# The last pair's feed-forward cut into two units, an earlier position table, masks that open the score banks, and new engine orders

## The chip, the cores and the metric

The kernel runs on one core of a Trainium2 chip. Its metric is the device time of one execution in microseconds (us); lower is better. A core has five engines that matter here, each with its own in-order instruction queue: TensorE (PE; its weight loads are shown as PEld), VectorE (DVE), ScalarE (ACT), GpSimd (POOL) and SyncE (SP), which only issues DMAs in this kernel. They meet through semaphores. PSUM has eight banks, into which PE writes and from which DVE and ACT read.

## The reference

Sixteen images of 3x96x96 are cut into 36 patches of 16x16, each projected to 256 features; with a class token and position embeddings this makes 37 tokens. 128 text tokens are appended: 165 tokens a sequence. Then one transformer block follows:

```
h = concat([cls, patches @ W_lin.T + b]) + pos ; h = concat([h, txt])      # (16, 165, 256)
# attention: 16 query heads, 4 key/value heads of 16; rope; |i - j| <= 32 only
h = h + softmax(mask(rope(q) @ rope(k).T / 4)) @ v @ Wo                    # on layernorm(h)
# feed-forward, both matmuls with per-token int8 activations and ternary weights
u = bit_linear(layernorm(h), w1)                                          # 256 -> 1024
u = silu(depthwise_conv1d(u, conv_w, conv_b))                             # 3 taps along the sequence
h = h + bit_linear(u, w2)                                                 # 1024 -> 256
```

The convolution couples each token of a sequence with its two neighbours; nothing couples two sequences. The second `bit_linear` scales each token by the largest of its 1024 values, so its down projection can only start when all 1024 features of the token are known.

## The kernel before

Two sequences make a pair: `T` = 330 tokens, as three tiles of `TT` = 110 rows. There are eight pairs (`PAIRS`). For each pair `n` the attention runs in 11 blocks `j` of 30 queries (`QB`): `scores` (two fp32r matmuls, L1817, and a bf16 mask matmul onto the edge columns, L1829, the last of the three), `max_s` on DVE (L1488), `shift` (L1837, subtracts the maximum), `exp` on ACT (L1259), `turn_p` (four transposes, L1846), `keep_p` on ACT (L1267) and `context` (eight matmuls into 32-column tiles, L1860). Two PSUM banks (`S_BANKS`) alternate over the blocks. After 4, 8 and 11 blocks, `turn_ctx`, `norm`, `select`, `keep_sel` and `out_proj` (L1887) make one tile of 110 tokens, and `add_att` adds it to `h` (L1504).

The feed-forward of pair `n` is: `var2`, `rstd2`, `norm2`, `max_x`, `quant_x`, `dequant_x` (normalise and quantise three tiles), `turn_xs` (six transposes), `high_x`, `low_x` (the operand as two fp32r halves), then eight chunks `m` of 128 hidden features: `up` (four matmuls of 330 columns, L1915 and L1916), `mid` on ACT (centre tap and bias, L1306), `left` and `right` on DVE (the outer taps, L1564 and L1571). Per four chunks: `tanh` on ACT, `silu` (L1578), `abs_g` on ACT, `fold_g` (L1588), `max_g`. Then `turn_max` (L1922), `scale2`, `spread` (L1927, the scale of each token to all partitions), `quant_g` (L1625, int8), `conv_g` on ACT (int8 to bf16, L1326), `down` (8 matmuls a tile, L1934), `add_ffn` (L1633) and `store`.

For pairs 0 to 6 `up` uses three banks in turn and `down` the same three, one a tile. The last pair uses four others for `up`, so that it need not wait for the banks; its `turn_xs` goes to `F_BANK` and `N_BANK`. `up` of chunk m waits until `right` of the chunk that had its bank before is done.

The order of the work on each engine is not worked out at run time. `ORDER` holds for every helper, pair and piece a tick; each engine runs its helpers by rising tick, in order. An item with a late tick sits behind all items with earlier ones, and what it waits for stalls all behind it. The feed-forward of pair n is interleaved in this way with the attention of pair n+1; the last pair's has nothing beside it but what is left of pair 6's. `ONCE` does the same for the start: the images' transposes (`turn_pix`), the patch projections (`patch`: 12 matmuls L1715 and one L1717 with the position table) and the weights' quantisation.

`patch(0)` stands behind a wait for `consts_in`, the DMA of all constants but the identity (132.5 KB). The last 164 of its columns, from `C_HOT`, are the one-hot rows that pick a position's row of `posb`.

Of the kernel before, what the change touches and what calls it, by code (L numbers as in the profile page):

```python
# [37 lines left out]
NT = 3  # L38
# [11 lines left out]
HALFC = MH // 2  # L50
K_PLACED = 16 * 2 * HKV
# [66 lines left out]

C_ID = 0
# [8 lines left out]
for _j in range(NB):  # L128
    if V_RUNS:
# [14 lines left out]
        (19, 21),  # L144
        (69, 73),
        (137, 142),
        (219, 223),
        (294, 300),
        (374, 381),
        (451, 454),  # L150
    ),
    'pe.project': (
        (7, 8, 10),
        (23, 28, 36),
        (77, 82, 89),
        (155, 159, 166),
        (230, 236, 243),
        (308, 312, 316),
        (384, 390, 399),
        (462, 469, 475),  # L160
    ),
    'pe.turn_q': (
        (12, 14, 17),
        (43, 51, 57),
        (106, 115, 125),
        (178, 187, 197),
        (257, 265, 278),
        (334, 344, 355),
        (408, 422, 430),
        (490, 498, 510),  # L170
    ),
    'pe.turn_k': (
        (15, 16),
        (60, 65),
        (129, 135),
        (201, 206),
        (284, 290),
        (361, 367),
        (440, 445),
        (513, 518),  # L180
    ),
    'pe.scores': (
# [8 lines left out]
    ),  # L191
    'pe.shift': (
# [8 lines left out]
    ),  # L201
    'pe.turn_p': (
# [8 lines left out]
    ),  # L211
    'pe.context': (
# [29 lines left out]
    'pe.out_proj': (
        (55, 79, 96),
        (124, 156, 172),
        (200, 225, 249),
        (276, 304, 327),
        (356, 380, 404),
        (433, 457, 480),
        (509, 538, 556),
        (578, 599, 609),  # L250
# [3 lines left out]
        (204,),  # L254
        (280,),
        (358,),
        (436,),
        (514,),
        (583,),
        (613,),  # L260
    ),
    'pe.up': (
# [8 lines left out]
    ),  # L271
    'pe.turn_max': (
        (176,),
        (253,),
        (328,),
        (406,),
        (484,),
        (558,),
        (610,),
        (624,),  # L280
# [3 lines left out]
        (260,),  # L284
        (337,),
        (413,),
        (492,),
        (563,),
        (611,),
        (625,),  # L290
    ),
    'pe.down': (
        (193, 194, 195),
        (270, 271, 272),
        (349, 350, 351),
        (425, 426, 428),
        (503, 504, 505),
        (572, 573, 574),
        (612, 614, 615),
        (626, 627, 628),  # L300
# [3 lines left out]
        (8,),  # L304
        (13,),
        (17,),
        (40,),
        (101,),
        (149,),
        (198,),  # L310
# [40 lines left out]
    ),  # L351
    'dve.norm': (
        (23, 34, 41),
        (48, 56, 82),
        (93, 106, 129),
        (142, 156, 180),
        (194, 203, 227),
        (240, 251, 277),
        (288, 298, 324),
        (337, 346, 367),  # L360
    ),
    'dve.add_att': (
        (29, 37, 44),
        (52, 76, 86),
        (100, 117, 135),
        (150, 176, 184),
        (200, 223, 233),
        (247, 271, 281),
        (295, 320, 330),
        (343, 361, 370),  # L370
# [3 lines left out]
        (87,),  # L374
        (136,),
        (185,),
        (234,),
        (282,),
        (332,),
        (372,),  # L380
# [3 lines left out]
        (94,),  # L384
        (143,),
        (192,),
# [3 lines left out]
        (377,),  # L390
    ),
    'dve.low_x': (
        (55,),
        (102,),
        (151,),
        (201,),
        (248,),
        (297,),
        (345,),
        (382,),  # L400
    ),
    'dve.left': (
# [8 lines left out]
    ),  # L411
    'dve.right': (
# [8 lines left out]
    ),  # L421
    'dve.silu': (
        (68, 79),
        (119, 128),
        (167, 178),
        (216, 226),
        (263, 275),
        (312, 322),
        (363, 369),
        (401, 402),  # L430
    ),
    'dve.fold_g': (
        (77, 83),
        (126, 132),
        (171, 181),
        (224, 230),
        (272, 279),
        (323, 327),
        (368, 373),
        (403, 405),  # L440
    ),
    'dve.max_g': (
        (81, 84),
        (130, 133),
        (174, 182),
        (228, 231),
        (274, 280),
        (325, 329),
        (371, 374),
        (404, 406),  # L450
    ),
    'dve.scale2': (
        (88,),
        (137,),
        (186,),
        (235,),
        (284,),
        (331,),
        (376,),
        (407,),  # L460
    ),
    'dve.quant_g': (
# [1557 lines left out]
```

## Time and profile before

| | |
|---|---|
| median of 3 runs | 415.74 us (414.12 to 416.45) |
| profiled execution, whole | 415.2 us |
| its span, first to last instruction | 413.4 us |
| busy | PE 352.1, DVE 304.9, ACT 256.1, POOL 213.2 us |
| mean granted TensorE clock | 0.94 of 2.4 GHz |

A group's mean duration of a matmul covers its whole way through the array; matmuls overlap, so the distance from one start to the next is what one costs in a stream. The slices of the page are a fortieth of the span each, some 10.3 us.

### The profile page before, as it was taken

The numbers are of one execution on the slowest core, as the hardware profiler recorded it, in microseconds if no ns is written. First come the engines' busy times: TensorE is split into PE (matmuls) and PEld (weight loads), VectorE is DVE, ScalarE is ACT, GpSimd is POOL, SyncE is SP. The second block draws the span as 40 slices with busy tenths as digits, with TensorE's granted clock in tenths as the row PEclk, the third lists the DMA queues.
The fourth block names the chain that finished last, engine by engine and source line by source line (L and its number), as shares of the span: only waits on it lengthen the run. The fifth ranks groups of instructions, "written<-read, shape, count | busy, mean of one in ns | idle before, by whom it ended". The sixth has DMA issues, their size and how long they took to land.

```text
span 413.4 us, 8175 instructions
## 1 busy us (share of the span) xinstructions
PE 352.1 (85%) x2920; PEld 270.8 (66%) x2920; DVE 304.9 (74%) x644; ACT 256.1 (62%) x481; POOL 213.2 (52%) x245
## 2 busy tenths in 40 slices
PE   1698789999999999999999999999999989737424
PEld 1375546777876796678667866896688667517304
DVE  2246567664699788878978899589869986985971
ACT  2222435658795788578767894788678765813721
POOL 5407489489559917981899059926960052010000
PEclk9979999999999999999999999999999999955956
DMA  7671601101100121012001201110111001000101
GB/s 238 147 178 41 215 19 33 33 11 26 22 14 2 32 52 32 2 36 55 11 1 25 61 18 32 35 27 9 32 36 35 0 2 35 0 0 2 33 1 33
DMA packets 21884, 16.69 MB, mean 40 GB/s; under 512 B 12413, under 2 KB 20914, under 8 KB 21843
## 3 DMA queue, kind: packets, MB, share of 16 engines
q1 hardware_dynamic: 20948, 15.11, 14.8%
q10 hardware_dynamic: 895, 1.06, 1.0%
q8 instruction: 23, 0.38, 0.4%
q14 instruction: 18, 0.15, 0.1%
HBM read 9.82 MB, written 3.38 MB: 32 GB/s over the span
## 4 chain that ended last, share of the span: by engine, by line
PE 68%; DVE 14%; ACT 8%; issue 6%; DMA 2%; ACTq 0%; DVEq 0%
PE bank L1817 7%; PE bank L1846 7%; PE bank L1766 6%; PE bank L1934 6%; PE bank L1860 6%; PE bank L1915 5%; PE bank L1715 4%; PE bank L1887 4%; PE bank L1916 4%; PE bank L1837 3%; PE bank L1878 2%; DMA cst<-in_consts 2%; DVE shared L1625 2%; PE bank L1829 2%; PE bank L1927 2%
## 5 line engine op out<-in xcount | busy, mean ns | idle before, releaser
L1267 ACT COPY pT<-bank 94x480 f32<-94x480 f32 (+3 forms) x88 | 48.4, 554 | 28.9 <-PE bank L1846 28.1
L1488 DVE TENSOR_REDUCE mx<-bank 120x4 fp32r<-120x376 f32 (+3 forms) x88 | 44.2, 505 | 29.9 <-PE bank L1829 29.2
L1817 PE MATMUL bank<-kbd,q_hl 128*120 128x376 f32 (+3 forms) x176 | 50.8, 373 | 5.9 <-ACT pT L1267 3.3
L1259 ACT ACTIVATE pr<-bank 120x376 f32<-120x376 f32 (+3 forms) x88 | 39.6, 455 | 25.3 <-PE bank L1837 24.6
L1846 PE MATMUL bank<-cst,pr 120*94 120x120 f32 (+3 forms) x352 | 51.1, 269 | 2.7 <-ACT pr L1259 2.2
L1107 POOL TENSOR_TENSOR rs<-ve,half_neg 110x3 f32<-110x3 f32 x16 | 16.6, 1040 | 65.1 <-DVE ve L1516 48.0
L1915 PE MATMUL bank<-xT_hi,w1T 128*128 128x330 f32 x128 | 42.9, 341 | 1.1 <-DVE late L1571 0.9
L1846 PEld LDWEIGHTS bank<-cst,pr 120*94 120x94 f32 (+3 forms) x352 | 36.3, 121 | 11.1 <-ACT pr L1259 6.7
L1129 POOL TENSOR_TENSOR rc<-qk,cst 110x320 f32<-110x320 f32 x22 | 20.7, 939 | 43.7 <-ACT qk L1230 42.7
L1114 POOL TENSOR_SCALAR xn<-h,mv,rs 110x256 f32<-110x256 f32 x21 | 26.5, 1272 | 26.5 <-PE bank L1754 26.1
L1916 PE MATMUL bank<-xT_lo,w1T 128*128 128x330 f32 x128 | 39.4, 314 | 0.0
L1860 PE MATMUL bank<-pT,vw 94*32 94x120 f32 (+3 forms) x704 | 37.4, 291 | 1.5 <-ACT pT L1267 1.4
L1837 PE MATMUL bank<-mx,neg_id 120*120 120x376 f32 (+3 forms) x88 | 36.2, 417 | 2.8 <-DVE mx L1488 2.4
L1766 PE MATMUL bank<-wqk,xnT 128*110 128x384 f32 x96 | 37.0, 510 | 0.3 <-ACT xnT L1223 0.3
L1817 PEld LDWEIGHTS bank<-kbd,q_hl 128*120 128x120 f32 x176 | 26.1, 182 | 15.8 <-ACT pT L1267 6.9
L1934 PE MATMUL bank<-w2T,shared 128*110 128x256 bf16 x192 | 26.9, 303 | 9.4 <-ACT shared L1326 9.4
L1934 PEld LDWEIGHTS bank<-w2T,shared 128*110 128x110 bf16 x192 | 24.7, 147 | 11.9 <-ACT shared L1326 11.6
L1326 ACT CAST shared<-shared 128x1320 bf16<-128x1320 int8 x16 | 20.4, 1296 | 16.7 <-DVE shared L1625 16.4
L1136 POOL TENSOR_TENSOR qkr<-rc,rsn 110x160 f32<-110x160 f32 x44 | 29.7, 695 | 1.7
L1860 PEld LDWEIGHTS bank<-pT,vw 94*32 94x32 f32 (+3 forms) x704 | 19.0, 146 | 17.7 <-issue 10.9
L1164 POOL TENSOR_SCALAR shared<-shared,am 110x256 f32<-110x256 f32 x21 | 23.8, 1144 | 5.6 <-ACT shared L1287 5.6
L1156 POOL TENSOR_SCALAR shared<-h,mv,rs 110x256 f32<-110x256 f32 x21 | 25.9, 1241 | 1.2 <-POOL rs L1107 1.1
(126 smaller groups left out, 863.9 us busy)
## 6 DMA issues: line engine op xcount, KB each, us to landing
out<-h SPq DMA_DIRECT2D x8, 330.0 KB
kbd<-shared SPq DMA_DIRECT2D x56, 41.2 KB, 2.1
wn<-in_w SPq DMA_DIRECT2D x2, 1024.0 KB, 6.6
shared<-in_x SPq DMA_DIRECT2D x4, 432.0 KB
h<-in_txt SPq DMA_DIRECT2D x1, 770.0 KB
late<-in_lin SPq DMA_DIRECT2D x1, 768.0 KB, 7.2
vw<-v_rows SPq DMA_DIRECT2D x8, 94.0 KB
v_rows<-qk SPq DMA_DIRECT2D x8, 82.5 KB
```

The lines of the kernel that those rows point to most:

```text
L1136: o = nc.gpsimd.tensor_tensor(qkr[:, e::2], rc[:, e::2], rsn[:, 1 - e::2], ALU.add)
L1259: nc.scalar.activation(pr[:, g % 3, 0:HKV * WIDTH[j]], S_BANKS[g % 2][0:QP, 0:HKV * WIDTH[j]], ACT.Exp, scale=HD ** -0.5).then_inc(exped, 1)
L1267: nc.scalar.copy(pT[0:WIDTH[j], g % 3, :], S_BANKS[g % 2][0:WIDTH[j], 0:HKV * QP]).then_inc(p_kept, 1)
L1488: nc.vector.tensor_reduce(mx[:, g % 4, :].bitcast(F32R), S_BANKS[g % 2][0:QP, 0:HKV * WIDTH[j]].rearrange("p (k c) -> p k c", k=HKV), axis ...
L1766: o = nc.tensor.matmul(qk_bank(n, t)[0:TT, 0:QKC + QK], xnT[:, k, t * TT:(t + 1) * TT], wqk[:, k, :], start=(k == 0), stop=(k == KD - 1))
L1817: nc.tensor.matmul(dst, q_hl[n % 2][:, j * QB:(j + 1) * QB, :].bitcast(F32R), kbd[n % 2][:, part, :, k0:k0 + w].bitcast(F32R), start=(part ...
L1837: nc.tensor.matmul(S_BANKS[g % 2][0:QP, 0:HKV * w], neg_id[:, :].bitcast(F32R), mx[:, g % 4, :].bitcast(F32R).unsqueeze(2).to_broadcast([Q ...
L1846: o = nc.tensor.transpose(S_BANKS[g % 2][0:w, kv * QP:(kv + 1) * QP], pr[:, g % 3, kv * w:(kv + 1) * w], ident[0:QP, 0:QP])
L1860: o = nc.tensor.matmul(C_BANK[VS * kv:VS * (kv + 1), col:col + QP], vw[n % 2][0:WIDTH[j], j, :, kv], pT[0:WIDTH[j], g % 3, kv * QP:(kv + 1 ...
L1915: nc.tensor.matmul(dst, w, xT_hi[:, k, :].bitcast(F32R), start=(k == 0), stop=False)
L1916: o = nc.tensor.matmul(dst, w, xT_lo[:, k, :].bitcast(F32R), start=False, stop=(k == KD - 1))
L1934: o = nc.tensor.matmul(down_bank(n, t)[0:TT, 0:D], gq[:, m, t * TT:(t + 1) * TT], w2T[:, m, :], start=(m == 0), stop=(m == MH - 1))
```

## The change

- `UNITS` = 9: pairs 0 to 6 are units 0 to 6; the last pair is units 7 and 8. Unit 7 is its first sequence: it normalises and quantises tiles 0 and 1 (220 tokens), computes `up` for 166 columns (165 and one more), convolves, gates and takes maxima over 165 tokens, and scales and quantises tile 0 (110 tokens). Unit 8 is the second: tile 2 is normalised, `up` again covers 166 columns, the gate 165 tokens, and tiles 1 and 2 (220 tokens) are quantised. All three `down` of the pair stay behind unit 8's `spread` in PE's order; the first waits only for unit 7's casts, the others for unit 8's.
- Banks: `up` of unit 6 has two banks instead of three, `down` of pair 6 uses two in turn, unit 7 has two banks (one of them `F_BANK`), unit 8 three. Units 7 and 8 turn their operands, maxima and scales in one bank each (`F_BANK`, `N_BANK`).
- Unit 7's normalisation and quantisation of two tiles is on POOL and ACT; before, the last pair's was on DVE.
- The last pair is stored tile by tile.
- `scores`: the mask matmul comes first and opens the bank (`start=True`), the two score matmuls add to it.
- The one-hot columns have a DMA of their own (37 rows of 656 bytes), second on ACT's queue; `patch` waits for it instead of `consts_in`.
- All of `ORDER` and `ONCE` are new.

```diff
-            pe.wait_ge(consts_in, 16)
+            pe.wait_ge(hot_in, 16)
...
             act.dma_start(cst[:, 0:C_REST], ident_d).then_inc(ident_in, 16)
+            act.dma_start(cst[0:POSR, C_HOT:C_END], hot_d).then_inc(hot_in, 16)
             act.dma_start(posb[:, :], pos_d).then_inc(pos_in, 16)
             act.dma_start(clsb[:, :, :], cls_d).then_inc(cls_in, 16)
-            act.dma_start(cst[:, C_REST:C_END], consts).then_inc(consts_in, 16)
+            act.dma_start(cst[:, C_REST:C_HOT], consts).then_inc(consts_in, 16)
...
+def tiles_of(u):
+    return range(NT) if u < LAST else (range(0, 2), range(2, NT))[u - LAST]
+def conv_of(u):
+    return (0, T) if u < LAST else ((0, SEQ), (SEQ, T))[u - LAST]
+def up_of(u):
+    return (0, T) if u < LAST else ((0, SEQ + 1), (SEQ - 1, T))[u - LAST]
+def gate_tiles(u):
+    return range(NT) if u < LAST else (range(0, 1), range(1, NT))[u - LAST]
...
-        def up_bank(n, m):
-            return Z_BANKS[m % 3] if n < PAIRS - 1 else (*S_BANKS, C_BANK, Z_BANKS[2])[m % 4]
+        def up_banks(u):
+            if u < LAST - 1:
+                return Z_BANKS
+            return (Z_BANKS[0:2], (Z_BANKS[2], F_BANK), (*S_BANKS, C_BANK))[u - LAST + 1]
...
         def down_bank(n, t):
-            return Z_BANKS[t] if n < PAIRS - 1 else (*Z_BANKS[0:2], S_BANKS[0])[t]
+            return Z_BANKS[t % 2 if n == LAST - 1 else t]
...
-                for part in range(2):
-                    nc.tensor.matmul(dst, q_hl[n % 2][:, j * QB:(j + 1) * QB, :].bitcast(F32R),
-                                     kbd[n % 2][:, part, :, k0:k0 + w].bitcast(F32R), start=(part == 0), stop=(part == 1))
...
                 nc.tensor.matmul(over, identb[0:QP, 0:QP], hide,
-                                 start=False, stop=True, skip_group_check=True).then_inc(scored, 1)
+                                 start=True, stop=False, skip_group_check=True)
+                for part in range(2):
+                    o = nc.tensor.matmul(dst, q_hl[n % 2][:, j * QB:(j + 1) * QB, :].bitcast(F32R),
+                                     kbd[n % 2][:, part, :, k0:k0 + w].bitcast(F32R), start=False, stop=(part == 1),
+                                     skip_group_check=True)
+                o.then_inc(scored, 1)
...
             def down(n, t):
-                pe.wait_ge(g_kept, NP * (n + 1))
-                if n == PAIRS - 1:
+                if n < LAST:
+                    pe.wait_ge(g_kept, NP * (n + 1))
+                    if n == LAST - 1 and t == 2:
+                        pe.wait_ge(ffn_added, NT * n + 1)
+                else:
+                    pe.wait_ge(g_kept, NP * (LAST + min(t, 1) + 1))
                     pe.wait_ge(ffn_added, NT * n)
...
+            def store_tile(t):
+                sp.wait_ge(ffn_added, NT * LAST + t + 1)
+                sp.dma_start(out_v[LAST][:, t, :], h[:, LAST, t, :]).then_inc(stored, 16)
```

The end of the new orders, by tick (in brackets the unit or pair and the piece). ACT: ... tanh(6,1), quant_x(7), keep_sel(7,2), abs_g(6,1), high_x(7), mid(7,0), mid(7,1), conv_g(6,0), conv_g(6,1), ... DVE: ... norm(7,2), fold_g(6,0), left(6,6), left(6,7), right(6,6), right(6,7), max_x(7), max_g(6,0), silu(6,1), add_att(7,2), var2(8), fold_g(6,1), max_g(6,1), norm2(8), low_x(7), scale2(6), left(7,0), max_x(8), quant_g(6,0), quant_g(6,1), ... PE: ... up(6,6), context(7,10), turn_ctx(7,2), up(6,7), select(7,2), out_proj(7,2), turn_xs(7), turn_max(6), up(7,0), up(7,1), spread(6), up(7,2), up(7,3), down(6,0), turn_xs(8), ... At the start, PE's `turn_pix` of the fourth load comes right after `turn_xn(0)`; before, three items later.

## Rows read from the trace of the kernel before

**Rows 1.** The page's slices: granted TensorE clock, tenths, 40 equal slices.
```profile
PEclk9979999999999999999999999999999999955956
```

**Rows 2.** Windows: per stretch the length, then each engine's busy us, PEclk, DMA share.
```profile
60.00:345.00 285.00, 273.51 (x2486) 213.32 (x2486) 229.06 (x476) 207.41 (x398) 182.35 (x209) 1.00 0.11 26
345.80:390.10 44.30, 28.44 (x186) 22.68 (x184) 37.01 (x81) 22.72 (x35) 1.40 (x1) 0.77 0.03 9
371.00:381.00 10.00, 6.14 (x31) 6.14 (x32) 6.03 (x12) 3.35 (x4) 0.00 (x0) 0.51 0.01 2
390.10:413.40 23.30, 6.80 (x29) 5.17 (x29) 11.90 (x18) 6.49 (x5) 0.00 (x0) 0.59 0.05 15
```

**Rows 3.** Waits of PE from 60 to 345 us: total us, times, longest.
```profile
PE bank L1817 <- ACT pT L1267: 2.6, 7, 0.6
PE bank L1837 <- DVE mx L1488: 2.4, 6, 0.7
```

**Rows 4.** The chain that ended last, at the start: start, us, what.
```profile
1.98 9.74 DMA cst<-in_consts
```

**Rows 5.** Timeline of DVE, 0 to 40 us: start, us, line, shapes, idle before.
```profile
8.89 0.92 DVE L1393 COPY wn<-bank 128x144 f32<-128x144 f32 x3 [2.03 <-PE bank L1702]
...
18.33 0.95 DVE L1388 COPY shared<-shared 72x768 f32<-72x768 f32 x1 [2.52 <-DMA shared<-in_x]
19.35 0.92 DVE L1393 COPY wn<-bank 128x144 f32<-128x144 f32 x3
```

**Rows 6.** Timeline of PE, 34 to 41 us.
```profile
37.14 2.83 PE L1715 MATMUL bank<-late,wn 128*126 128x256 f32 x12 [1.10 <-issue]
```

**Rows 7.** Timeline of PE in the body, two stretches.
```profile
60.68 0.44 PE L1860 MATMUL bank<-pT,vw 94*32 94x120 f32 x8
61.05 1.54 PE L1766 MATMUL bank<-wqk,xnT 128*110 128x384 f32 x4
...
115.99 0.65 PE L1860 MATMUL bank<-pT,vw 94*32 94x120 f32 x16
116.57 0.49 PE L1817 MATMUL bank<-kbd,q_hl 128*120 128x248 f32 x2
```

**Rows 8.** Groups by form, weight loads: busy us, mean ns, idle before.
```profile
L1817 PEld LDWEIGHTS bank<-kbd,q_hl 128*120 128x120 f32 x176 | 26.1, 182 | 15.8 <-ACT pT L1267 6.9 <-issue 4.0 <-ACT q_hl L1236 2.0
L1829 PEld LDWEIGHTS bank<-mask_sb,identb 120*120 120x120 bf16 x88 | 11.6, 132 | 0.0
```

**Rows 9.** Groups by form, DVE.
```profile
L1564 DVE SCALAR_TENSOR_TENSOR shared<-bank,conv,shared 128x328 f32<-128x328 f32 x32 | 17.2, 553 | 2.9 <-ACT shared L1306 2.8
L1578 DVE SCALAR_TENSOR_TENSOR late<-wn,late 128x1320 f32<-128x1320 f32 x8 | 12.2, 1539 | 0.0
```

**Rows 10.** Timeline of all engines, last pair's attention end and first `up`.
```profile
362.92 0.42 DVE L1504 TENSOR_TENSOR h<-bank,h 110x256 f32<-110x256 f32 x1 [0.77 <-PE bank L1887]
...
380.88 0.40 PE L1915 MATMUL bank<-xT_hi,w1T 128*128 128x330 f32 x1
```

**Rows 11.** Timeline of all engines, from the last `right` to the last addition.
```profile
389.11 1.01 DVE L1571 SCALAR_TENSOR_TENSOR late<-bank,conv,late 128x328 f32<-128x328 f32 x2
...
396.41 0.89 PE L1922 MATMUL bank<-cst,shared 128*110 128x128 f32 x3 [8.61 <-DVE shared L1599]
...
398.90 1.47 PE L1927 MATMUL bank<-shared,ones 110*128 110x330 f32 x2 [1.60 <-DVE shared L1615]
400.40 2.97 DVE L1625 TENSOR_TENSOR shared<-late,bank 128x1320 int8<-128x1320 f32 x2 [1.56 <-PE bank L1927]
401.96 2.73 ACT L1326 CAST shared<-shared 128x1320 bf16<-128x1320 int8 x2 [7.60 <-DVE shared L1625]
404.75 4.44 PE L1934 MATMUL bank<-w2T,shared 128*110 128x256 bf16 x24 [4.38 <-ACT shared L1326]
...
409.23 0.48 DVE L1633 SCALAR_TENSOR_TENSOR h<-bank,am,h 110x256 f32<-110x256 f32 x1 [0.39 <-PE bank L1934]
```

**Rows 12.** DMA, 409 to 414 us: busy tenths of the 16 engines in 40 slices.
```profile
DMA  0000000000003586566667676553100000000000
```

More of the change, by code:

```diff
@@ L115, in tok_tiles, with pair_of, rows_of, tokens_of @@
     return [s for s in range(TOKT) if any(p[2] == n for p in tok_pieces(s))]
+def pair_of(u):
+    return min(u, LAST)
+def tiles_of(u):
+    return range(NT) if u < LAST else (range(0, 2), range(2, NT))[u - LAST]
+def rows_of(u):
+    return slice(tiles_of(u).start, tiles_of(u).stop)
+def tokens_of(u):
+    return slice(TT * tiles_of(u).start, TT * tiles_of(u).stop)
+def conv_of(u):
[4 more added lines that the diff above has]
+    return range(NT) if u < LAST else (range(0, 1), range(1, NT))[u - LAST]
+def gate_rows(u):
+    return slice(gate_tiles(u).start, gate_tiles(u).stop)
+def gate_tokens(u):
+    return slice(TT * gate_tiles(u).start, TT * gate_tiles(u).stop)
+def before(u):
+    return min(u, LAST)
 C_ID = 0
@@ L160 @@
-        (462, 469, 475),
+        (7, 9, 10),
+        (25, 28, 33),
+        (71, 76, 81),
+        (148, 155, 167),
+        (223, 226, 239),
+        (303, 309, 317),
+        (378, 388, 395),
+        (455, 463, 471),
     ),
     'pe.turn_q': (
[L163 to L170, printed above, removed]
+        (11, 16, 17),
+        (43, 54, 57),
+        (90, 97, 114),
@@ L171 @@
+        (174, 184, 189),
+        (245, 258, 264),
+        (323, 338, 341),
+        (409, 416, 419),
+        (474, 488, 495),
     ),
     'pe.turn_k': (
[L173 to L180, printed above, removed]
+        (14, 15),
+        (59, 62),
+        (118, 127),
+        (201, 204),
+        (267, 278),
+        (352, 358),
+        (425, 431),
+        (500, 509),
     ),
     'pe.scores': (
[8 rows of a table removed]
[8 rows of a table added]
@@ L245 @@
[L245 to L250, printed above, removed]
+        (51, 87, 100),
+        (126, 151, 172),
+        (200, 232, 251),
+        (280, 306, 327),
+        (354, 391, 406),
+        (432, 465, 486),
+        (512, 539, 555),
+        (580, 596, 609),
     ),
@@ L283 @@
         (182,),
[L284 to L287, printed above, removed]
+        (259,),
+        (335,),
+        (414,),
+        (490,),
         (563,),
-        (611,),
-        (625,),
+        (614,),
+        (634,),
+        (636,),
     ),
     'pe.down': (
[L293 to L300, printed above, removed]
+        (195, 197, 198),
+        (270, 272, 275),
+        (348, 350, 351),
+        (427, 428, 429),
+        (503, 505, 507),
+        (574, 576, 578),
+        (617, 620, 622),
+        (637, 638, 639),
     ),
@@ L303 @@
         (4,),
-        (8,),
+        (9,),
         (13,),
[L306 to L310, printed above, removed]
+        (24,),
+        (37,),
+        (83,),
+        (119,),
+        (177,),
     ),
@@ L373 @@
         (45,),
[L374 to L378, printed above, removed]
+        (90,),
+        (139,),
+        (188,),
+        (236,),
+        (284,),
         (332,),
-        (372,),
+        (360,),
+        (374,),
     ),
@@ L389 @@
         (338,),
-        (377,),
+        (370,),
+        (381,),
     ),
     'dve.low_x': (
-        (55,),
-        (102,),
-        (151,),
+        (54,),
+        (103,),
+        (150,),
         (201,),
         (248,),
-        (297,),
-        (345,),
-        (382,),
+        (296,),
+        (346,),
+        (378,),
+        (393,),
     ),
     'dve.left': (
[8 rows of a table removed]
[9 rows of a table added]
     ),
     'dve.right': (
[8 rows of a table removed]
[9 rows of a table added]
     ),
     'dve.silu': (
[L423 to L430, printed above, removed]
+        (69, 81),
+        (117, 130),
+        (166, 178),
+        (214, 226),
+        (261, 275),
+        (312, 323),
+        (361, 372),
+        (396, 411),
+        (427, 428),
     ),
     'dve.fold_g': (
[L433 to L440, printed above, removed]
+        (75, 84),
+        (120, 133),
+        (174, 183),
+        (224, 231),
+        (272, 278),
+        (322, 327),
+        (365, 375),
+        (403, 415),
+        (429, 431),
     ),
     'dve.max_g': (
[L443 to L450, printed above, removed]
+        (77, 86),
+        (129, 134),
+        (179, 184),
+        (227, 232),
+        (274, 279),
+        (324, 329),
+        (371, 376),
+        (412, 418),
+        (430, 432),
     ),
@@ L686 @@
         (39,),
-        (46,),
+        (47,),
         (53,),
+        (56,),
+        (59,),
+        (62,),
+    ),
+    'pool.norm2': (
+        (16,),
+        (24,),
+        (32,),
+        (40,),
+        (48,),
+        (54,),
         (57,),
-        (),
+        (60,),
     ),
     'pool.dequant_x': (
-        (17,),
-        (25,),
-        (33,),
+        (18,),
+        (26,),
+        (34,),
         (41,),
-        (48,),
+        (49,),
         (55,),
         (58,),
-        (),
+        (61,),
     ),
@@ L1084, in _ @@
                     store(n)
-            sp.wait_ge(stored, 16 * PAIRS)
+                for t in work["store_tile"].get(q, ()):
+                    store_tile(t)
+            sp.wait_ge(stored, 16 * (LAST + NT))
         @block.gpsimd
@@ L1154, in norm2 @@
                 pool.wait_ge(rstd2, n + 1)
-                for t in range(NT):
+                for t in tiles_of(n):
                     o = nc.gpsimd.tensor_scalar(xn2[:, t, :], h[:, n, t, :], mv2[:, t, 0:1], rs2[:, t:t + 1],
@@ L1162, in dequant_x @@
                 pool.wait_ge(x_rounded, n + 1)
-                for t in range(NT):
+                for t in tiles_of(n):
                     o = nc.gpsimd.tensor_scalar(xn2[:, t, :], xn2[:, t, :], MAGIC, am1[:, 3, t:t + 1],
@@ L1285, in quant_x @@
                 act.wait_ge(scale1, n + 1)
-                for t in range(NT):
+                for t in tiles_of(n):
                     o = nc.scalar.activation(xn2[:, t, :], xn2[:, t, :], ACT.Identity, bias=magic[0:TT, :],
@@ new lines, in abs_g, with conv_g @@
+            def abs_g(u, p):
+                ms, cols = slice(HALFC * p, HALFC * (p + 1)), slice(*conv_of(u))
+                act.wait_ge(silued, NP * u + p + 1)
+                nc.scalar.activation(th[:, ms, cols], gates[before(u) % 2][:, ms, cols], ACT.Abs).then_inc(absed, 1)
+            def conv_g(u, p):
+                ms, cols = slice(HALFC * p, HALFC * (p + 1)), gate_tokens(u)
+                act.wait_ge(g_scaled, NP * u + p + 1)
+                if u:
+                    act.wait_ge(down_done, NT * before(u))
+                nc.scalar.copy(gq[:, ms, cols], g8[:, ms, cols]).then_inc(g_kept, 1)
@@ L1627, in quant_g @@
+            def quant_g(u, p):
+                ms, cols = slice(HALFC * p, HALFC * (p + 1)), gate_tokens(u)
+                dve.wait_ge(scale_spread, u + 1)
+                if u:
+                    dve.wait_ge(g_kept, NP * (before(u) - 1) + p + 1)
+                nc.vector.tensor_tensor(g8[:, ms, cols], gates[before(u) % 2][:, ms, cols],
+                                        spread_at(u).unsqueeze(1).to_broadcast([128, HALFC, cols.stop - cols.start]),
                                         ALU.mult).then_inc(g_scaled, 1)
@@ L1917, in up, with turn_max @@
                 o.then_inc(up_done, 1)
-            def turn_max(n):
-                pe.wait_ge(g_maxed, n + 1)
-                for t in range(NT):
-                    o = nc.tensor.transpose(xs_bank(n, 0)[0:TT, t * 128:(t + 1) * 128], gm[:, 2, t * TT:(t + 1) * TT], ident)
+            def turn_max(u):
+                pe.wait_ge(g_maxed, u + 1)
+                for i, t in enumerate(gate_tiles(u)):
+                    o = nc.tensor.transpose(max_at(u)[:, i * 128:(i + 1) * 128], gm[:, 2, t * TT:(t + 1) * TT], ident)
```

720 lines of the change are left out of this document (368 added, 352 removed), and 180 rows, old and new, of the table ORDER.

## The prediction

> **What bounds the kernel now.** The page's slices and the windows come first, and they split the run into three stages. From 60 to 345 us PE is busy 273.5 of 285 us at full clock, DVE 229.1 and ACT 207.4 [rows 2]: PE's queue is the bound, and a microsecond taken off PE there, or an earlier start of that stage, shows in full. The waits say how little slack there is: 13 waits, 5.0 us, on the score banks and maxima [rows 3]. The chain of waits then gives the start: the first patch projection is released at 11.8 us by the constants' DMA, issued at 1.98 [rows 4]. The end is another matter: from 345.8 us to 390.1, where the last `right` ends, DVE is busy 37.0 of 44.3 us and PE 28.4; after it 23.3 us of steps follow one another, each on one engine, with PE's clock at 0.59 [rows 2]. The clock had fallen to 1.2 GHz (0.51) in the stretch from 371 to 381 [rows 2], after the slices before had shown PE with gaps [rows 1]. The last pair's attention was added at 362.9 and its first `up` ran at 380.9 [rows 10]: 18 us in which pair 6's feed-forward was finished and the last pair's normalised on the same DVE.
>
> **The start.** `patch(0)` also needs the pixels, whose last copy ends at 9.8 [rows 5], and the DMA now before it is a fifth of the size; so it can start at 9.8 instead of 11.8, 2.0 us earlier. Not all of it lasts: the third load's pixels arrive at 18.3, their sort ends at 19.3, and the transposes that waited for the second load's copy until 20.3 [rows 5] can be only 1.0 us earlier. Further on PE stood 1.10 us before the fourth patch projection [rows 6], waiting for copies of pixels that it had turned two projections too late; `turn_pix` of the fourth load is now ahead of those projections, so that wait goes. Sum -2.1 us. The new DMA is one more issue ahead of the others of ACT's queue; what waits for the shortened constants now (POOL's first power, DVE's rope, the copies of K) runs after 20 us and is covered. SP's fourth token move goes ahead of the second pair's K: no wait hangs on that for 20 us. Bounds: 0 (if the second load's chain absorbs it) and -3.5 (if DVE's first ropes, behind the same copies, also move up).
>
> **The body.** A `context` alone takes 0.37 us to the next start (60.68 to 61.05), two in a row 0.58 (115.99 to 116.57) [rows 7]: 0.16 saved by each that follows another. Counting the ticks, the 88 contexts of PE stand in 78 runs before and in 69 after: 9 x 0.16 = 1.4 us. Mask first: where nothing hides the first weight load of a block (after a wait or after a `context`), what stands open is the mask's 0.13 us instead of the scores' 0.18 [rows 8]. At most 88 x 0.05 = 4.4 us; I take a quarter, 1.1 us, about the share of blocks that come after a wait or a `context`. The matmuls themselves are the same, and the maximum waits for the third of three either way. Below zero this could go the other way by as much, if the fp32r loads come to stand behind a mask too short to hide them (0.18 less the mask's own pass). The rest of the order is a reshuffle; nine more changes into fp32r matmuls, and some new waits, are set at +0.5. Sum -2.0 us; bounds -5.8 (4.4 + 1.4) and +4.
>
> **The end, DVE's work.** A 328-column tap takes 0.553 us, a 1320-column operation 1.539: 0.99 ns a column. Two taps take 1.01 [rows 9, 11], so one follows the other after 0.46, of which 0.33 is columns and 0.13 fixed. What DVE must do between 345.8 and the last `right` changes thus: 16 more taps at 0.13, +2.1; unit 7's gate and scale, formerly after the last `right`, now before it: two `silu` of 660 columns (0.79 each), two folds of 330 (0.46), three maxima of 165 (0.3), and the scale chain, 1.5 as between 397.3 and 398.9 in [rows 11]: +4.9; a second set of small statistics and two more `low_x`, +1.2; two tiles' normalising and quantising go to POOL and ACT, six operations of 256 columns at some 0.3, -1.9. Together +6.3: 37.0 + 6.3 = 43.3, and the last `right` cannot end before 389.1. The idle time decides: DVE had 7.3 us of it. Unit 7's taps can fill the wait for `spread`, casts and `down` of pair 6, but new waits come. `up` of pair 6 has two banks, so a chunk starts only after the trip `up`, ACT, two taps of the chunk two before. And ACT's queue holds `quant_x(7)` ahead of `keep_sel(7,2)`: the last attention tile cannot be projected before DVE has reached `max_x(7)`, behind all of pair 6's taps; `out_proj`, `add_att(7,2)`, unit 8 and, on DVE, pair 6's own maxima queue behind it. I take 6.0 us idle, near the 7.3 of now: last `right` at 395.1. Ends: 0 idle (389.1) and 10.3 (399.4, all round trips at the low clock).
>
> The Trainium skill, "VectorE: DVE Perf Modes", section "The TRN2 errata — SBUF-src ops pay a fixed extra latency per instruction", speaks against cutting: a big tile pays the fixed part once, small ones each time, and about 150 cycles of 0.96 GHz, 0.156 us, are measured there. By it the 16 taps would be 2.5 us instead of 2.1. The case's rows agree to 0.03 us.
>
> **The end, after the last `right`.** Before, from 390.1 [rows 11]: gate 6.3, `turn_max` 0.9, scale 1.6, `spread` 1.5, `quant_g` 3.0, last cast 1.3, `down` 4.5, addition 0.5, store and end 3.7: 23.3. After, for one sequence: gate 3.5 (1.6 + 0.7 for ACT's `abs` + 0.5 + 0.6), `turn_max` 0.65, scale 1.4, `spread` of 220 columns 1.0, `quant_g` 2.0, cast 0.9, `down` 16 instead of 24 at 4.44 / 24 = 0.185 (the first tile's run during the quantising) 3.0, addition 0.5. The last store's packets are under way from 410.5 to 412.6 [rows 12]; a third of the bytes leaves 0.7 of 2.1, so 2.3 instead of 3.7. Sum 15.2. Bounds: 14.2 (3.7 shrinks in proportion) and 16.6 (it stays).
>
> The skill's "DMA: Bandwidth & Descriptors", section "Anatomy of one DMA — SWDGE (gpsimd) path", has a fixed part of about 2.0 us plus the bytes at 436 GB/s; by it 220 KB less save 0.5 us, not 1.4, and the end would be 0.9 later. That fit is for another path than SP's; the rows show the packets alone taking 2.1 us for 330 KB.
>
> **Sum.** The end: 395.1 + 15.2 = 410.3 against 413.4, -3.1. With -2.1 and -2.0 the span is 406.2. The profiled execution took 1.8 us more than its span (415.2), and the runs' median lies 0.5 above it: 406.2 + 1.8 + 0.5 = 408.5.
>
> **The rivals.**
> - *The two units wait for each other.* Idle of 10.3 us in DVE; the end gives 399.4 + 15.2 = 414.6, +1.2 instead of -3.1, and 415.7 - 2.1 - 2.0 + 1.2 = 412.8. For it: the low clock of the last slices, the single queue entry on ACT. Against: with unit 7's `up` beside pair 6's `down` PE has fewer gaps and may hold 2.4 GHz.
> - *Start and body give nothing:* the earlier patch meets another wait, the merged contexts cost what they save. 415.7 - 3.1 = 412.6. For it: three arrivals of pixels bound the start anyway.
> - *Slower: the new order makes PE wait in the body.* The order after often puts two blocks' scores, then two shifts, then two transposes together; each bank then waits for its round through DVE and ACT. A wait of that kind now costs 0.38 us (5.0 / 13) [rows 3]. One more in 30 of the 88 blocks is +11.4: 419.9. It decides from 24 waits more (9.3 / 0.38, which eats the gain of 7.2 and 2.1 more). Against: DVE and ACT have 56 and 78 us free there.
> - *DVE fills every gap:* 389.1 + 15.2, -9.1 at the end: 402.5.
>
> **How the numbers follow.** 0.5%, 2.1 us, is what a measurement tells from no change. Chances: the forecast 0.52; units that wait 0.20 (half of that still faster, half the same); start and body nothing 0.12 (two thirds faster, one third the same); slower order 0.12; all gaps filled 0.04. Faster 0.52 + 0.04 + 0.10 + 0.08 = 0.74, same 0.14, slower 0.12. The range runs from near the filled-gap case to just past the two at 413: 403 to 416.
>
> **What would show it.** `patch(0)` at 9.8, not 11.8, and the first `scores` some 2 us earlier. The stage from 60 to 345 with contexts in pairs, and no more waits of L1817 and L1837 than 13. `up` of unit 7 before `down` of pair 6, DVE idle near 6 us from 345.8 to the last `right`, that at 395 less 4.1 for the shift of start and body. Then 15 us to the end. Wrong: `keep_sel(7,2)` over 5 us after `select`, PE idle over 20 us between 60 and 345, or a last store as long as before.

## The result and the profile after

The changed kernel takes 424.38 us (424.00 to 424.58, 4 runs) against 416.10 beside it: a ratio of 1.0211, 95% interval 1.0179 to 1.0243. The forecast was 408.5, the range 403 to 416: wrong in sign, and outside the range. The profiled execution took 424.0 us, its span 422.2, 8.8 more than before. Medians of before on the chips of the experiments below were 415.1 to 415.6. One execution each of e11 and e13 ran far slower (1109.65 and 502.55 us); medians and ratios leave it out, and of e13, whose profile is that execution (granted clock 0.645), only the first microseconds are read.

Three milestones split the 8.8: the first `scores` (block 0 of pair 0), the first `up` of unit 6, and the end of the span.

| us | before | after | shift | of it in this stage | predicted |
|---|---|---|---|---|---|
| first `scores` | 47.62 | 54.67 | +7.05 | +7.05 | -2.1 |
| `up` of unit 6 | 346.75 | 357.37 | +10.62 | +3.6 | -2.0 |
| end of the span | 413.4 | 422.2 | +8.8 | -1.8 | -3.1 |

**The start.** The chain of waits after, which answers to [rows 4]: start, us, what.
```profile
1.71 17.13 DMA posb<-in_pos
```
The timeline of PE has the first projection behind it, 7.2 us later than 11.82. The wait for the constants, which the change took out, was replaced by one for the position table, whose own line the change had not touched.
```profile
19.04 4.98 PE L1840 MATMUL bank<-late,wn 128*72 128x256 f32 x12 [9.00 <-DMA posb<-in_pos]
...
44.69 2.77 PE L1840 MATMUL bank<-late,wn 128*126 128x256 f32 x12
```
The last of these rows is the fourth projection: the 1.10 us ahead of it [rows 6] are gone, as foreseen, but the first `scores` still come 7.05 later, only 0.17 less than the first projection's 7.22.

The list of DMA issues in the first 25 us, of after: KB, median us to landing.
```profile
wqk<-in_wqk ACTq DMA_DIRECT2D x1, 384.0 KB, 17.2
cst<-in_consts ACTq DMA_DIRECT2D x1, 50.5 KB, 16.8
```
The constants were 132.5 KB before and took 9.7 us; with 50.5 KB they take 16.8. The semaphore and packet records of the trace say why. A DMA raises its semaphore in steps. Those of 37 rows (`hot`, `posb`) have one step at their issue and a single one when they land, as has the small `clsb`; the large ones have 13 to 16. So the 37 rows move as one share, and a large DMA in many; which DMA engine has a share the trace doesn't say. Before, `posb` was the first such one of ACT's queue: its packets run from 4.4 to 9.2 us. After, `hot` runs from 4.5 to 8.6 and `posb` starts when it is done, 8.7 to 18.3.

What stands behind them is held back in one share only. Of the 16 steps of the constants, 15 have come by 8.3 us in both kernels. The last comes at 11.7 before and at 19.2 after, each time right behind `posb` (10.2 and 18.8) and `clsb` (10.5 and 19.0). So the constants' landing at 11.7, from which the prediction started, was set by the 37-row `posb` ahead of them and not by their own 132.5 KB: e3, with both tables at 48 rows, has all 16 steps by 9.5 us.

**The body.** Windows of after: the body, and the two parts of the end (as [rows 2]).
```profile
60.00:345.00 285.00, 269.53 (x2426) 206.90 (x2424) 223.43 (x470) 203.77 (x392) 186.59 (x212) 1.00 0.11 25
356.40:405.60 49.20, 34.78 (x217) 27.79 (x215) 42.72 (x109) 28.88 (x50) 8.39 (x6) 0.72 0.03 8
405.60:422.20 16.60, 7.38 (x28) 5.54 (x28) 9.19 (x20) 5.23 (x7) 0.00 (x0) 0.58 0.07 20
```
PE is idle 15.5 of 285 us instead of 11.5. From one milestone to the next (2558 and 2564 matmuls recorded) busy is +0.7 and idle +2.9. The window of before:
```profile
47.60:346.70 299.10, 285.39 (x2558) 220.62 (x2558) 236.62 (x496) 213.18 (x410) 191.41 (x220) 0.99 0.12 30
```
and of after:
```profile
54.70:357.40 302.70, 286.07 (x2564) 220.10 (x2564) 234.18 (x496) 214.67 (x413) 196.36 (x220) 0.99 0.13 31
```
PE's waits from 60 to 345 us of after are, beside those of [rows 3]:
```profile
PE bank L1973 <- ACT pr L1367: 2.6, 6, 0.8
PE bank L1951 <- ACT pT L1375: 2.4, 7, 0.6
PE bank L2051 <- DVE shared L1720: 1.6, 2, 1.3
PE bank L1964 <- DVE mx L1600: 1.4, 5, 0.5
PE bank L2056 <- DVE shared L1737: 1.2, 2, 0.6
```
The two kinds that the slower rival named, the score banks and the maxima, are 12 waits and 3.8 us: one and 1.2 us fewer than before. What is new is `turn_max` and `spread` (L2051, L2056), 2.8 us in four waits for the feed-forward's fold and scale on DVE; before has none there. `context` did get cheaper, by 1.9 us (the prediction: 1.4). Its group by line, before:
```profile
L1860 PE MATMUL bank<-pT,vw 94*32 94x120 f32 (+3 forms) x704 | 37.4, 291 | 1.5 <-ACT pT L1267 1.4
```
and after:
```profile
L1987 PE MATMUL bank<-pT,vw 94*32 94x120 f32 (+3 forms) x704 | 35.5, 289 | 0.0
```

**The end.** From `up` of unit 6 to the last `right` it is 48.3 us after, 43.4 before; from there to the end 16.6 and 23.3. The closing chain on the timeline of all engines, against [rows 11]:
```profile
404.96 0.67 DVE L1691 SCALAR_TENSOR_TENSOR late<-bank,conv,late 128x164 f32<-128x164 f32 x2
...
409.48 0.67 PE L2051 MATMUL bank<-cst,shared 128*110 128x128 f32 x2 [4.58 <-DVE shared L1720]
...
411.49 1.10 PE L2056 MATMUL bank<-shared,ones 110*128 110x220 f32 x2 [1.34 <-DVE shared L1737]
...
412.63 2.05 DVE L1747 TENSOR_TENSOR shared<-late,bank 128x880 int8<-128x880 f32 x2 [0.67 <-PE bank L2056]
413.74 1.91 ACT L1436 CAST shared<-shared 128x880 bf16<-128x880 int8 x2 [1.18 <-DVE shared L1747]
...
415.69 3.66 PE L2068 MATMUL bank<-w2T,shared 128*110 128x256 bf16 x16 [1.14 <-ACT shared L1436]
...
419.39 0.48 DVE L1758 SCALAR_TENSOR_TENSOR h<-bank,am,h 110x256 f32<-110x256 f32 x1 [1.22 <-PE bank L2068]
```
Ahead of it stand the wait for `keep_sel(7,2)` that "What would show it" named, and one for unit 7's bank. PE's timeline of after:
```profile
374.43 2.04 PE L2014 MATMUL bank<-wo_sb,ctxP 128*110 128x256 f32 x4 [4.29 <-ACT ctxP L1389]
...
387.15 0.51 PE L2044 MATMUL bank<-xT_hi,w1T 128*128 128x166 f32 x1 [3.36 <-DVE late L1691]
```

### The profile page after: what moved, and what is told of

The parts are those of the page before. It is cut to its first block, busy times and chain, and to the rows that moved or that the text cites. A ratio compares the mean times of both kernels' runs of the same rounds, so it can differ in the third digit from the quotient of the medians.

```text
span 422.2 us, 8332 instructions
## 1 busy us (share of the span) xinstructions
PE 359.7 (85%) x2954; PEld 275.8 (65%) x2954; DVE 305.1 (72%) x675; ACT 261.9 (62%) x499; POOL 224.5 (53%) x250
## 4 chain that ended last, share of the span: by engine, by line
PE 48%; DVE 19%; POOL 9%; issue 8%; ACT 8%; DMA 5%; SPq 2%; ACTq 0%; DVEq 0%; POOLq 0%
PE bank L1891 6%; PE bank L1973 5%; PE bank L2068 4%; PE bank L1840 4%; DMA posb<-in_pos 4%; PE bank L2044 4%; PE bank L1954 3%; PE bank L2045 3%; PE bank L1987 3%; PE bank L2014 3%; DVE mx L1600 2%; DVE late L1691 2%; DVE late L1685 2%; POOL qkr L1242 2%; PE bank L1964 2%
## 5 line engine op out<-in xcount | busy, mean ns | idle before, releaser
L2044 PE MATMUL bank<-xT_hi,w1T 128*128 128x330 f32 (+1 forms) x144 | 50.7, 360 | 7.2 <-DVE late L1691 5.9
L1367 ACT ACTIVATE pr<-bank 120x376 f32<-120x376 f32 (+3 forms) x88 | 39.8, 455 | 24.1 <-PE bank L1964 23.3
L2045 PE MATMUL bank<-xT_lo,w1T 128*128 128x330 f32 (+1 forms) x144 | 45.4, 323 | 0.0
L1235 POOL TENSOR_TENSOR rc<-qk,cst 110x320 f32<-110x320 f32 x22 | 23.7, 1079 | 31.4 <-ACT qk L1337 29.8
L2044 PEld LDWEIGHTS bank<-xT_hi,w1T 128*128 128x128 f32 x144 | 29.6, 205 | 13.4 <-DVE late L1691 8.6
L1242 POOL TENSOR_TENSOR qkr<-rc,rsn 110x160 f32<-110x160 f32 x44 | 33.8, 789 | 1.7
L2045 PEld LDWEIGHTS bank<-xT_lo,w1T 128*128 128x128 f32 x144 | 29.9, 208 | 0.7
L1213 POOL TENSOR_TENSOR rs<-ve,half_neg 110x3 f32<-110x3 f32 (+2 forms) x9 | 9.2, 1026 | 39.4 <-DVE ve L1629 39.4
L1951 PE MATMUL bank<-mask_sb,identb 120*120 120x232 bf16 (+3 forms) x88 | 25.4, 288 | 5.4 <-ACT pT L1375 2.4
L2014 PE MATMUL bank<-wo_sb,ctxP 128*110 128x256 f32 x96 | 26.2, 396 | 4.4 <-ACT ctxP L1389 4.3
L1416 ACT ACTIVATE late<-bank,conv 128x330 f32<-128x330 f32 (+1 forms) x40 | 22.4, 571 | 11.2 <-PE bank L2045 10.8
```

What stands on the lines that cost most here:

```text
L1242: o = nc.gpsimd.tensor_tensor(qkr[:, e::2], rc[:, e::2], rsn[:, 1 - e::2], ALU.add)
L1367: nc.scalar.activation(pr[:, g % 3, 0:HKV * WIDTH[j]], S_BANKS[g % 2][0:QP, 0:HKV * WIDTH[j]], ACT.Exp, scale=HD ** -0.5).then_inc(exped, 1)
L2044: nc.tensor.matmul(dst, w, xT_hi[:, k, z0:z1].bitcast(F32R), start=(k == 0), stop=False)
L2045: o = nc.tensor.matmul(dst, w, xT_lo[:, k, z0:z1].bitcast(F32R), start=False, stop=(k == KD - 1))
```

## The experiments

Ratios are to before on the same chip, with 95% intervals; milestones are from each profile.

| | median | ratio | `scores` | `up` 6 | end |
|---|---|---|---|---|---|
| before | 415.1 to 416.1 | 1 | 47.6 | 346.7 | 413.4 |
| after | 424.38 | 1.0211 [1.0179, 1.0243] | 54.7 | 357.4 | 422.2 |
| e1 | 423.57 | 1.0180 [1.0137, 1.0224] | 54.4 | 356.2 | 422.8 |
| e2 | 416.88 | 1.0034 [1.0011, 1.0057] | 47.5 | 350.1 | 415.0 |
| e3 | 415.15 | 0.9992 [0.9973, 1.0011] | 45.7 | 348.8 | 413.3 |
| e4 | 414.09 | 0.9955 [0.9937, 0.9973] | 46.5 | 345.9 | 412.5 |
| e5 | 415.73 | 1.0015 [0.9992, 1.0038] | 45.8 | 348.8 | 413.3 |
| e6 | 411.44 | 0.9918 [0.9889, 0.9948] | 44.3 | 342.9 | 409.6 |
| e7 | 418.38 | 1.0082 [1.0052, 1.0112] | 44.3 | 346.9 | 414.7 |
| e8 | 412.12 | 0.9933 [0.9907, 0.9959] | 46.5 | 346.1 | 410.7 |
| e9 | 410.70 | 0.9896 [0.9869, 0.9923] | 44.2 | 344.1 | 408.5 |
| e10 | 411.36 | 0.9901 [0.9879, 0.9924] | 46.5 | 345.8 | 409.9 |
| e11 (e4 again) | 413.86 | 0.9949 [0.9924, 0.9973] | 47.1 | 346.4 | 412.6 |
| e12 (e6 again) | 412.01 | 0.9911 [0.9888, 0.9935] | 46.0 | 343.8 | 409.9 |
| e13 | 415.68 | 0.9997 [0.9972, 1.0022] | | | |
| e14 | 418.39 | 1.0074 [1.0043, 1.0104] | 47.4 | 350.6 | 415.2 |
| e15 | 418.04 | 1.0069 [1.0045, 1.0092] | 44.8 | 350.2 | 415.1 |

### The table: e1 to e4, e13, e14

e1 and e4 are the kernel before with the one-hot columns in a DMA of their own, as in the change. e2 is after with a single DMA for all constants. e3 is after, and e4 that e1, with both small tables padded to 48 rows:

```diff
-            act.dma_start(cst[0:POSR, C_HOT:C_END], hot_d).then_inc(hot_in, 16)
+            act.dma_start(cst[0:48, C_HOT:C_END], hot_d).then_inc(hot_in, 16)
...
-        posb = sb("posb", [POSR, D])
+        posb = sb("posb", [48, D])
```

> The kernel before, with one part of the change: the one-hot columns as a DMA of 37 rows ahead of the position rows. Theory (a DMA of 37 rows runs on a single DMA engine, so the second such DMA queues behind the first on it): the position rows land near 19 us instead of 10.2, the first patch projection starts near 19 instead of 11.8, and some 7 us are lost: 422 to 424. Rival (the loss is in the new orders, the late landing was chance traffic): first patch at 10 to 12, time 414 to 416.

> The kernel after without the separate table: all constants in one DMA as before, all else as after. Theory: first patch at 11.8, 424.4 less about 7 = 417 to 418; what is left against 416 is the orders' body loss less the tail's gain. Rival: 423 to 425, unchanged.

> The kernel after, with the one-hot columns and the position rows sent as 48 rows each (11 rows of padding), which divides over 16 DMA engines. Theory: both land by 8 us, the first patch starts at 9.8 to 10.5 when the pixels are there, and the time is 8 to 9 us under 424.4: 415 to 416.5. Rival: 423 to 425.

> The kernel before with the separate table, both small DMAs as 48 rows. Theory: first patch at about 10 instead of 11.8; 1 to 2 us gained on 416: 414 to 415. Rival (pixel arrivals bound the start anyway): 416.

The extra DMA alone makes the kernel before as slow as after. Its chain of waits has the same first link, and its first `scores` come 6.7 us later:
```profile
1.71 16.38 DMA posb<-in_pos
```
In e3 the first projection starts at 10.2, released by DVE's copy of the pixels, which is what the prediction had expected of the change itself (9.8). e2, without the extra DMA, takes 416.88, just under the 417 to 418 expected, and 0.3% more than before. Padding is worth 2.2% in either kernel; e3 equals before, and e4 is 0.45% faster. PE's timeline of e3:
```profile
10.24 4.87 PE L1840 MATMUL bank<-late,wn 128*72 128x256 f32 x12 [1.11 <-DVE wn L1503]
```

e13 pads only `posb`, e14 only `hot`.

> after with the one-hot table in 37 rows and the position table in 48. By the theory that 37 rows run one behind another on a single DMA engine and the cost comes from two such tables in sequence, the one-hot table lands at 9.5 as in after, the position table on 16 engines at about 9 to 10, patch(0) starts at 10.3, and the time is e3's, 415. Rival: what the busy engine holds of its share delays the second table too: the position table and patch(0) at 11 to 13, the time 416 to 418.

> The reverse: one-hot table in 48 rows, position table in 37. By the theory the position table lands at about 10.5, as in the kernel before, where it was the only such one ahead of the constants (10.2), and the time is 415. By the rival, that the bytes a row decide (1024 here, 656 there), it lands at 15 to 18 as in after, and the time is 420 to 424.

PE's timeline of e13:
```profile
10.03 4.88 PE L1840 MATMUL bank<-late,wn 128*72 128x256 f32 x12 [1.22 <-DMA posb<-in_pos]
```
and of e14:
```profile
13.19 4.41 PE L1840 MATMUL bank<-late,wn 128*72 128x256 f32 x12 [4.32 <-DMA posb<-in_pos]
```
A 37-row `hot` alone costs nothing, as the theory said. A 37-row `posb` alone costs 3 us by the medians: it lands at 13.0, though in the kernel before it landed at 10.2. Both theories missed this size. Only the two in sequence give 18.8.

### The order and the cut: e7, e8, e15

e7 keeps everything of e3 but the units: the last pair is one unit again, each of its pieces at the tick of unit 8. e8 keeps units, banks and mask of e3 and takes before's order for all that begins before 343 us there.

> The kernel after (48 rows, mask first, new orders) with the last pair's feed-forward in one unit again: row 7 of each feed-forward helper at the ticks of unit 8, banks and the single store as before. e3 less e7 is what the cut into two units brings with the order held. If the cut is worth what the tail gained (about 1.9 us) it takes 417; if the cut is worth the prediction's shorter closing chain (8 us less the DVE work put ahead of it) more, up to 421; if the tail's gain is the order's and not the cut's, 415. The body, 60 to 345 us, is expected as in e3: if the body's loss of 3.4 us came with the units or the banks of unit 6, it would be gone here, and up of unit 6 would start 3 us earlier than e3's 348.8.

> The kernel after (48 rows, mask first, two units with their banks) with the orders of before for every piece that begins before 343 us in before's trace, and the new orders for the rest. If the body's loss is the new order's, it takes 414.1 less the tail's 1.9, 412.2, and up of unit 6 starts at 345 as in e4; it is then faster than both kernels. If the loss came with the banks or the mask, the body stays 3 us long: 415. If the tail's gain depends on how the new order enters it, 414.

e7 has e3's long body, 302.6 us between the milestones against 303.1: units and banks don't cause it. In e8 the same stage is 299.6, like e4's 299.4. The window of e8:
```profile
46.50:346.10 299.60, 285.40 (x2564) 220.23 (x2564) 237.37 (x497) 214.34 (x413) 191.07 (x220) 0.99 0.12 30
```
and of e3:
```profile
45.70:348.80 303.10, 286.19 (x2564) 219.99 (x2564) 233.70 (x496) 214.51 (x413) 196.36 (x220) 0.99 0.13 31
```
So the body's loss is the new order's: idle 14.2 against 16.9 us. e3 has the four waits for `turn_max` and `spread` again (2.8 us), e8 has none of them. The end is 64.5 us in e3, 64.6 in e8, 67.8 in e7, 66.6 in e4. e8's time is the one expected (412.2), and e7's lies between its 417 and 421. With the new order held, the cut into two units is worth 3.3 us at the end (23.0 less 16.6 of closing chain, against DVE work put ahead of it); against the end of before and of e4 it is 2.0 to 2.2.

In before's order the cut's gain does not show in the whole time. e6 and e12 below have the 48 rows and the mask first, but neither cut nor new order, and take 411.44 and 412.01 us where e8 takes 412.12 (e6 on the same chip as e8). From the first `scores` to the end it is 365.3, 363.9 and 364.2 us: e8's shorter end goes with a body 1.0 and 1.8 us longer than theirs, and no run says why.

> As e8, but before's order only for what begins before 148 us in before's trace, the new order behind it. If 2.6 of the body's 3.4 us are lost between the first two units' up, as the stage starts of e3 and e4 say, up of unit 6 starts 0.8 after e8's (346.9) and the time is 412.9. Rival: each order only moves the lost microseconds from stage to stage, PE's queue having to meet the same hand-overs of the later units: up of unit 6 at 348.5 and 414.5 or more.

e15 answers less than it should. Where the two orders meet, PE stands 3.7 us for a maximum, which neither kernel has:
```profile
162.96 0.37 PE L1411 MATMUL bank<-mx,neg_id 120*120 120x248 f32 x1 [3.69 <-DVE mx L1047]
```
Its body is 305.4, that is 5.8 above e8's; without the seam's 3.7, 2.1 of the 3.5 are lost behind 148 us too. The forecast of 0.8 is refuted. The rival's numbers (348.5 and 414.5 or more) are nearer to 350.2 and 418.04, but with the seam in them they don't show it, and where exactly the order loses stays open.

### The mask: e5, e6, e11, e12

e5 is e3 with the mask matmul last, e6 is e4 with it first. e11 and e12 repeat e4 and e6 in one set of rounds.

> The kernel after with both small tables as 48 rows (e3: 415.15), and in scores the mask matmul last again, as in the kernel before; nothing else. The prediction gave 1.1 us to the mask's new place (a quarter of 88 x 0.05), so by it e5 takes about 416.2, and PE between 60 and 345 us is busy or waiting 1 us longer. Rival: the first weight load of a block is hidden anyway, and the two are the same within 0.4. A third, from the prediction's lower bound: the fp32r loads stand open behind a short mask, and e5 is faster than e3.

> The kernel before with its table split off and both small tables as 48 rows (e4: 414.09), and in scores the mask matmul first; orders, units and banks are those of before. Same question as e5, in the other order of work: by the prediction 413.0, by the rival 414.1; slower than 414.5 if the fp32r loads lose their cover.

> e4 once more (before, split table, 48 rows, mask last), on the chip and in the rounds of its partner e12, so that the mask's place is read without the scatter between jobs: 0.4% below before, 414.

> e6 once more (the same with the mask first). In e6's profile the stage from the first scores to the first up of unit 6 was 0.8 us shorter than e4's, its start 2.2 us earlier. If the mask's place is worth what the prediction said, e12 is 1.1 below e11; if all of e6's 2.6 us hold, 2.6 below; if e6 had a lucky start, equal.

By the ratios mask first gains 0.2% in after's order (e3, e5) and 0.4% in before's (e4, e6 and again e11, e12); the intervals of each two overlap. e5 (415.73) lies between the two expected times, e6 (411.44) below the 413.0, and e12 is 1.9 us under e11. In the profiles the stage from first `scores` to `up` of unit 6 gains 0.0 (e5 to e3), 0.8 (e4 to e6) and 1.5 us (e11 to e12). The prediction's 1.1 lies among them. In after's order PE's busy time falls by 1.3 us (287.5 to 286.2), but its idle time rises by as much. The mechanism shows in the groups of weight loads (busy us, mean ns, idle before): what waits for a bank at a block's head is now the mask's load of 131 ns, not the scores' of 182, and 1.0 us less is idle before it. e11's scores:
```profile
L1822 PEld LDWEIGHTS bank<-kbd,q_hl 128*120 128x120 f32 x176 | 26.1, 182 | 15.7 <-ACT pT L1270 6.9 <-issue 3.9 <-ACT q_hl L1238 2.0
```
and e12's mask:
```profile
L1831 PEld LDWEIGHTS bank<-mask_sb,identb 120*120 120x120 bf16 x88 | 11.5, 131 | 14.7 <-ACT pT L1270 7.0 <-issue 4.2 <-ACT q_hl L1238 2.0
```
The profiles' starts differ by up to 2.9 us in kernels with the same start. They go with the granted clock from 18 to 30 us: 0.72 in e4, e8, e10 and e11 (first `scores` at 46.5 to 47.1), 0.86 in e6 and e12 (44.3, 46.0), 1.00 in e9 (44.2). That part of e6's gain is not the mask's. The clock is not all of it, since e6 and e12 differ by 1.7 us at 0.86.

### The end's waits: e9, e10

e9 is e8 with `keep_sel(7,2)` ahead of `quant_x(7)` on ACT. e10 also has `right(7,0)` ahead of `max_x(8)` on DVE.

```diff
-ACT ... quant_x(7), keep_sel(7,2), ...
+ACT ... keep_sel(7,2), quant_x(7), ...
```

> e8 (412.12) with one item moved: on ACT keep_sel(7,2) ahead of quant_x(7). In e8 out_proj(7,2) stands 4.3 us behind that copy, as the prediction feared. If this wait is on the path, DVE's 1.7 us wait for out_proj goes, the last pair's additions and unit 8's operand come earlier, and the time falls by 1.5 to 2: 410.4. Rival: DVE's own queue (taps, gate and quantising of pair 6) is what the closing chain waits for, and the moved copy changes nothing beyond 0.5.

> e9 and one more item moved: on DVE right(7,0) ahead of max_x(8). In e8 it stands behind both quant_g of unit 6 and so up(7,2) waits 3.4 us for its bank. By the theory that the two-bank rule of unit 7 is on the path, up of unit 7 runs through and about 1 us more is won: 409.4. Rival: DVE has the same work in any order and is the bound there; 0 more than e9.

`out_proj` comes 1 us earlier, but the end from `up` of unit 6 on is 64.6, 64.4 and 64.1 us in e8, e9 and e10. PE's timeline of e10:
```profile
361.91 2.04 PE L1461 MATMUL bank<-wo_sb,ctxP 128*110 128x256 f32 x4 [3.32 <-ACT ctxP L836]
...
375.09 0.51 PE L1491 MATMUL bank<-xT_hi,w1T 128*128 128x166 f32 x1 [3.04 <-DVE late L1138]
```
Each move leaves most of its wait in place: the 4.3 us become 3.3, the 3.4 become 3.0. Neither forecast (1.5 and 1) holds in the profiles; the rival (DVE has the same work in any order) does, within 0.5. e9's median, 410.70, is near the 410.4 expected, but that is no hit: its lower ratio (0.9896 against e8's 0.9933, intervals overlapping) came with an earlier start in its profile, so no gain of e9 over e8 is shown. It is still 1.0% below before and the lowest ratio here, level with e10 and e12.

## Why the prediction was wrong

**The start: the step that failed.** It is the sentence "the DMA now before it is a fifth of the size; so it can start at 9.8 instead of 11.8". It priced a DMA by its bytes and counted the new one as "one more issue". The wait for `posb` stood in the code beside the one that was taken out, and the prediction has no row for its landing (10.2 before, against 11.7 for the constants). What the runs showed in its place: the 37-row DMAs move one behind the other in a single share, and a second one put ahead of `posb` brings it in at 18.8. The term was -2.1 and measured +7.05: a miss of 9.2 of the 16.0 us between the predicted span (406.2) and the measured one; the body has 5.6 of them and the end 1.3. e1 shows it alone (first `scores` +6.7), e3 undoes it. The bounds, 0 and -3.5, had no end on the slow side. With 48 rows the step is nearly right: 10.2 for 9.8.

The Trainium skill, "DMA: Bandwidth & Descriptors", section "Why a DMA increments its semaphore by 16 and not by 1", has the rule that would have warned: a copy is spread over k engines, the largest k up to 16 that divides the outermost size on both sides, and 127 rows get one engine. 37 is prime as well. This case's trace agrees: one step of the semaphore at the landing of each 37-row table, 16 for each table of 48 rows.

**The body: -2.0 predicted, +3.6 measured.** The merged contexts came (1.9 for 1.4). The mask's place, sized at 1.1, gave 0.0 in this order (e5 to e3) and 0.8 and 1.5 in before's. The term that failed is "nine more changes into fp32r matmuls, and some new waits, are set at +0.5". With -1.9 and 0.0 for those two, it has to hold 5.5 us. e8 agrees: it is 3.5 us shorter than e3 though it lacks the merged contexts, so the new order loses 3.5 + 1.9 = 5.4 without them. The rival "PE waits in the body" had the right place and sign but another price and other waits: not the score banks, but `turn_max` and `spread`, which wait for DVE. Its 24 more waits did not come; four of 0.7 us did.

**The end: -3.1 predicted, -1.8 measured.** DVE's work up to the last `right` was sized well: 42.7 us busy and 6.5 idle, forecast 43.3 and 6.0, and the last `right` came 4.9 later against `up` of unit 6, forecast 5.0. The closing chain took 16.6 and not 15.2. That this is its upper bound is chance: the bound was for a last store as long as before, and the store came in as forecast. Of the 1.4, 0.7 is `down`: 16 matmuls took 3.66 us and not 3.0. The price of 0.185 each was a mean over two clocks: the clock rose at 408.1, and the matmuls before it start 0.21 us apart, the last seven 0.11. The stream of 24 ran at a granted 0.62:
```profile
404.75:409.20 4.45, 4.44 (x24) 4.19 (x24) 0.97 (x2) 0.00 (x0) 0.00 (x0) 0.62 0.00 0
```
After, the shorter stream ended while the clock was still at 1.2 GHz:
```profile
415.70:419.40 3.70, 3.65 (x16) 3.24 (x16) 0.49 (x2) 0.00 (x0) 0.00 (x0) 0.50 0.18 50
```
That is 0.229 each: the eight matmuls taken away were, in time, the cheap ones. e12, with 24 matmuls at the low clock throughout, pays 0.224 each:
```profile
400.40:405.80 5.40, 5.37 (x24) 4.95 (x24) 0.97 (x2) 0.00 (x0) 0.00 (x0) 0.50 0.00 0
```
Of the rest of the 1.4, 0.3 is in the gate, 0.1 in `spread`, and what is left between the steps. The last addition's end to the end of the span is 2.3, as forecast: the packets of the last store, a third of the bytes, are under way for 0.8 us instead of 2.1.

**The rivals.** None of the four had the start. That the units wait for each other is refuted (idle 6.5, not 10.3), and so is a DVE that fills every gap. "Start and body give nothing" (412.6) comes nearest to what the change does without its table's fault, e3's 415.2. The gains in the contexts and the closing chain exist in their stages, and that of the mask in before's order; the new order spends them. Without it the mask and the 48 rows are shown to bring 0.8 to 0.9% (e6, e12); that the cut adds to this is not shown.

## What to carry to other kernels

- Before a DMA is split or added, count the shares (steps of its semaphore) in which it lands and what stands behind it; a 23.7 KB table of 37 rows ahead of another cost 7 us, and 11 rows of padding gave it back.
- Where two semaphores release one instruction, look up the landing of both; when the later one goes, the other sets the price.
- A cut, a mask's place and an order are separable: put the order of before under the new code and time each alone.

## What was not expected of the hardware

- A 37 KB table of 37 rows landed at 10.2 us with the 132.5 KB constants behind it, at 13.0 with a 48-row table ahead of it, at 18.8 with a 37-row one ahead. Fifteen of the constants' 16 shares were in by 8.3 us even then; only the last waited. The engine that takes all its rows presumably carries its share of the pixels and weights as well, which no run here took away.
- A shorter stream of matmuls at the end is not shorter in proportion: 24 took 4.44 us at a granted 0.62, 16 took 3.65 at 0.50, because the clock rose only within the longer one; in e12 it did not rise, and 24 took 5.37.
- The clock granted between 18 and 30 us differs between executions of kernels with the same start (0.72, 0.86, 1.00), and the first `scores` with it, by up to 2.9 us.
